# Expert feedforward: router logits written with tokens on partitions, x stationary and the router's columns moving

## The reference, cut to what matters

```python
gate_base = xf @ Wg.T
up_base = xf @ Wu.T
base_out = silu(gate_base) * up_base @ Wd.T
router_logits = xf @ Wr.T                       # (tokens, 8)
probs = softmax(router_logits, axis=-1)
topw, topi = top_k(probs, 2)
...
h = silu(gate_base + g_lora) * (up_base + u_lora)   # for each expert
acc + (h @ Ad_e.T @ Bd_e.T * SCALING) * we[:, None]
```

## Time and profile before

| | |
|---|---|
| time, median of three runs | 2139.03 us (2136.92 to 2142.73) |
| the profiled execution, its own time | 2141.15 us |
| its span, first to last instruction | 2139.4 us |
| mean granted TensorE clock | 0.915 of 2.4 GHz |
| PE busy | 1819.8 us, 85% |
| PEld busy | 1374.9 us, 64% |
| DVE busy | 1452.1 us, 68% |
| ACT busy | 956.3 us, 45% |
| POOL busy | 509.6 us, 24% |

### The profile page before, as it was taken

The page is one execution under the profiler, slowest core; times in us unless marked ns, Lnnn a source line. Parts: engine busy times, 40 slices in busy tenths (PEclk is TensorE's granted clock), DMA queues, the critical chain, the costliest instruction groups (busy, mean ns, idle before and its releaser), DMA issues. The chain is left out here.

```text
span 2139.4 us, 32688 instructions
## 1 busy us (share of the span) xinstructions
PE 1819.8 (85%) x12270; PEld 1374.9 (64%) x12270; DVE 1452.1 (68%) x2729; ACT 956.3 (45%) x1614; POOL 509.6 (24%) x503
## 2 busy tenths in 40 slices
PE   4489999765668999999999985999997799857886
PEld 2256665213448999999999975777875577623443
DVE  8478887694745566566566554566665677648997
ACT  3436666402314444444444432433443211259995
POOL 5233331270010010010000001001100388723422
PEclk9679999656889999999999997999998999978998
DMA  5598894217622122222221214211211311030000
GB/s 157 51 98 96 96 97 45 99 66 230 205 79 57 55 64 69 75 67 63 80 72 56 67 48 162 104 70 40 90 60 54 118 50 50 21 123 6 20 22 34
DMA packets 117568, 166.53 MB, mean 78 GB/s; under 512 B 13536, under 2 KB 67680, under 8 KB 115104
## 3 DMA queue, kind: packets, MB, share of 16 engines
q1 hardware_dynamic: 110756, 151.85, 29.9%
q10 hardware_dynamic: 6656, 12.58, 1.6%
HBM read 117.91 MB, written 21.05 MB: 65 GB/s over the span
## 5 line engine op out<-in xcount | busy, mean ns | idle before, releaser
L1583 ACT ACTIVATE f_gate<-f_gu 128x256 f32<-128x256 f32 x264 | 98.2, 381 | 274.3 <-PE f_gu L1449 187.1
L1711 DVE TENSOR_TENSOR f_hid<-f_gate,f_gu 128x256 f32<-128x256 f32 x264 | 108.2, 420 | 162.6 <-ACT f_gate L1583 159.7
L567 DVE TENSOR_REDUCE a_rowmax<-a_ring 128x2 f32<-128x512 f32 x256 | 164.9, 687 | 51.7 <-PE a_ring L649 49.4
L2525 PE MATMUL e_py<-e_kv,e_toep 128*128 128x320 f32 x640 | 174.5, 436 | 7.5 <-DVE e_kv L2549 7.5
L2525 PEld LDWEIGHTS e_py<-e_kv,e_toep 128*128 128x128 f32 x640 | 122.7, 192 | 59.0 <-issue 9.1
L520 ACT ACTIVATE a_prob<-a_sT 128x1024 f32<-128x1024 f32 x128 | 130.6, 1026 | 48.0 <-PE a_sT L638 48.0
L1462 PE MATMUL f_gu<-f_lowh,f_bg 128*128 128x256 f32 x704 | 141.3, 283 | 5.2 <-POOL f_lowl L1368 4.9
L1449 PE MATMUL f_gu<-f_xhi,f_wg 128*128 128x256 f32 x704 | 130.5, 283 | 0.0
L1449 PE MATMUL f_gu<-f_xhi,f_wu 128*128 128x256 f32 x704 | 129.1, 281 | 0.0
L1716 DVE TENSOR_TENSOR f_hl<-f_hid,f_hh 128x768 fp32r<-128x768 f32 (+2 forms) x90 | 84.5, 939 | 55.9 <-ACT f_hh L1629 54.8
L1462 PEld LDWEIGHTS f_gu<-f_lowh,f_bg 128*128 128x128 f32 x704 | 115.6, 191 | 9.7 <-POOL f_lowl L1368 5.2
(11 more groups left out here) (420 smaller groups left out, 4853.5 us busy)
## 6 DMA issues: line engine op xcount, KB each, us to landing
f_entry<-in_WdT SPq DMA_DIRECT2D x89, 256.0 KB
d_staging<-in_w SPq DMA_DIRECT2D x16, 1024.0 KB, 5.5
a_qs<-a_hi SPq DMA_DIRECT2D x64, 128.0 KB, 7.2
a_ks<-a_hi SPq DMA_DIRECT2D x64, 128.0 KB, 6.2
e_toep<-lags SPq DMA_DIRECT2D x32, 256.0 KB, 3.1
f_entry<-in_Bg SPq DMA_DIRECT2D x89, 64.0 KB
f_entry<-in_Bu SPq DMA_DIRECT2D x89, 64.0 KB
cf<-in_xT SPq DMA_DIRECT2D x4, 1024.0 KB, 7.8
```

The source lines that it names most:

```text
L567: dve.tensor_reduce(rowmax[:, s % 2, :, e * SLOTS + j], ring[n % RING][:, :].rearrange("p (q t) -> p q t", t=T), AX.X, ALU.max, negate=Tru ...
L1583: act.activation(gate[:, i % 2, :], gu[n % 3][:, 0, :], ACT.Silu).then_inc(s_["gate_ready"], 1)
L1711: dve.tensor_tensor(hid[:, j, :], gate[:, i % 2, :], gu[n % 3][:, 1, :], ALU.mult).then_inc(s_["hid_ready"], 1)
L2525: last = pe.matmul(py[n % RING][:, 0:DIAG * BS], toep[:, h % 3, (t - j) * P:(t - j + 1) * P], kv[:, h % 2, :, j, :], start=(j == 0), stop= ...
```

## The change

`logits` now writes the 16 columns with tokens on partitions at once: for each half q of the block and each k, the stationary operand is the 128x128 piece of `raw_x` and the moving one is `wr[:, k, :]` with its 8 columns. `turn_logits`, `fetch_logits`, the tile `f_logitT`, the item "lgT" of the bank's order and the semaphores `lgT_done` and `lgT_ready` go. `logits` stays where it was (s = 3, and ahead of base(0) in the first block); `route_start` stays at s = 5. `grow` waits for `lg_done` where it waited for `lgT_done`.

```diff
-    PREPARE = ("x0", "x1", "lgT", "lg", "z0", "z1", "mk0", "mk1", "low")
+    PREPARE = ("x0", "x1", "lg", "z0", "z1", "mk0", "mk1", "low")
...
                 def logits(b):
-                    claim("lgT", b)
+                    claim("lg", b)
                     pe.wait_ge(s_["raw_ready"], (b + 1) * TB)
-                    for k in range(KT):
-                        last = pe.matmul(misc[0:E_, 0:T], wr[:, k, :], raw_x[:, k, :], start=(k == 0), stop=(k == KT - 1))
-                    last.then_inc(s_["lgT_done"], 1)
-
-                def turn_logits(b):
-                    claim("lg", b)
-                    pe.wait_ge(s_["lgT_ready"], b + 1)
                     for q in range(TB):
-                        last = pe.matmul(misc[:, q * E_:(q + 1) * E_], logitT[:, q * P:(q + 1) * P],
-                                         keep["ident"][0:E_, 0:E_], start=True, stop=True)
+                        for k in range(KT):
+                            last = pe.matmul(misc[:, q * E_:(q + 1) * E_], raw_x[:, k, q * P:(q + 1) * P], wr[:, k, :],
+                                             start=(k == 0), stop=(k == KT - 1))
                     last.then_inc(s_["lg_done"], 1)
...
                 logits(0)
                 base(0)
-                turn_logits(0)
                 base(1)
...
                     if ahead and s == 3:
                         logits(b + 1)
-                    if ahead and s == 4:
-                        turn_logits(b + 1)
...
-                def fetch_logits(b):
-                    act.wait_ge(s_["lgT_done"], b + 1)
-                    act.activation(logitT[:, :], misc[0:E_, 0:T], ACT.Copy).then_inc(s_["lgT_ready"], 1)
-                    act.wait_ge(s_["lgT_ready"], b + 1)
-                    act.sem_inc(s_["misc_read"], 1)
...
                 x_raw(0, 1)
-                fetch_logits(0)
...
-                    if ahead and s == 4:
-                        fetch_logits(b + 1)
...
                 def grow(b):
                     dve.wait_ge(s_["lo_ready"], b + 1)
-                    dve.wait_ge(s_["lgT_done"], b + 1)
+                    dve.wait_ge(s_["lg_done"], b + 1)
```

More of the change, by code:

```diff
@@ L1316, in expert_feedforward @@
         weigh = mk.sb("f_weigh", [P, 2, 2, T])
-        logitT = mk.sb("f_logitT", [E_, T])
         route = mk.sb("f_route", [P, 8, TB * E_])
@@ L1333, in expert_feedforward @@
         raw_low = raw[:, :].rearrange("p (j w t) -> p j w t", j=2, w=2)
-        names = ("rank_made", "x_turned", "raw_ready", "hi_ready", "lo_ready", "misc_read", "lgT_done", "lgT_ready", "lg_done",
+        names = ("rank_made", "x_turned", "raw_ready", "hi_ready", "lo_ready", "misc_read", "lg_done",
                  "lg_ready", "exp_ready", "route_steps", "grown_ready", "masks_turned", "masks_ready", "a_done", "low_ready",
```

## The result

The changed kernel takes 2131.28 us (median of nine runs, 2126.22 to 2133.42), where the kernel before took 2136.92 us over its nine runs (2132.50 to 2142.73); the ratio is 0.9971, with a 95% interval of 0.9958 to 0.9984. Measured again with two other sets of runs it was 0.9958 (0.9943 to 0.9973) and 0.9961 (0.9949 to 0.9973). So 6 to 9 us are gained, 0.29% to 0.42% of the time, where 4.7 us and most likely "within 0.3%" were forecast. The profiled execution took 2133.42 us.

What follows compares the result with a forecast made beforehand. PE was taken to bound the kernel in the later blocks; -4.0 us there and -0.7 in the first block sum to -4.7, from the median of 2139.03 to 2134.4 us, range 2131 to 2140, about 8 in 10.

Steps and rivals of the forecast that it cites:

- PE sets the pace of the seven later blocks: From 655 to 1270 us PE is busy 612.3 of 615 us; what it no longer issues comes off the time.
- `turn_logits` costs 0.62 us: Later blocks: distance from `base` to `down` 0.74 us with it, 0.12 without; removal saves 4.3 us over seven blocks.
- `logits` after: 1.87 us from its first record to `down`, 0.05 more than before: Later blocks: 16 records, 0.11 us apart, take 1.87 us against 1.82; 0.35 us more for seven blocks.
- The first block: -0.7 us: First token block: +0.1 for `logits` at half clock, -0.62 for `turn_logits`, -0.17 for the wait ahead of `turn_masks`.
- the clock rises later: First block: short records don't help raise the clock, base(0) runs slow longer; costs 1.7 us, 2136.0 us; chance 0.22.
- both bounds of the unknown cost: New `logits`, per record: 0.11 us (the loads' pace) or 0.25 us (each waits out the one before); 0.11 taken.
- nothing arriving: The 4.7 us are lost again at a later wait; 2139.0 us; chance 0.10.
- Short records that wait for each other: New `logits`: records adding to the same columns need 0.25 us each; 18 us more, 2152 us; chance 0.05.
- a clock that falls in the later blocks: Short records bring a clock dip of 3.4 us in each of seven blocks; 24 us in all, 2158; chance 0.05.
- moving columns alone: New `logits`: 8 moving columns set the pace, 0.4 us for 1.9; 10 us more than the sum, 2124; chance 0.03.
- A dip less: The shifted start escapes the clock dip from 646 to 656 us; 3.4 us go, 2131 us; chance 0.05.
- The load's time: First block: loads follow the clock, 0.22 us at half, 0.11 at full, against the page's 107 ns whatever the clock.

Runs made afterwards that it cites:

- the short group: Changed kernel with 24 fp32 matmuls (48 records of 8 moving columns, results overwritten) added ahead of the stage's first transpose; one run, 2128.99 us.
- the probe with 8 columns loaded: Changed kernel with two fp32 matmuls added ahead of `down` in four steps, loads 8x128, 128x128, 64x128, 128x8 (this one at s = 0); one run, 2147.75 us.
- padding with zeros: Kernel before, old logits form, router's columns padded from 8 to 128 and logits' rows from 8 to 128; 0.9979 of before.

## Why the prediction came out as it did

- **PE sets the pace of the seven later blocks.** Right. What PE lost in its records came off the steps to 0.02 us, no later wait took it back, and removing ACT's copy and moving nothing else left the other steps alike.
- **`turn_logits` costs 0.62 us.** The step that failed first: the measure ended at the first record of `down`. Its second record was late as well, by 0.11 us, and the cost was 0.73 us, 0.8 us more over seven blocks. The timeline of before had this row.
- **`logits` after: 1.87 us from its first record to `down`, 0.05 more than before.** The mis-sized term, and the larger miss. The pace of 0.11 us a record was right (fourteen distances of 0.11), but the ends of the group were taken from `turn_logits`: the gap of 0.21 us ahead of it, 0.13 between its first two records and 0.18 behind the last. They belong to its load of 8 rows. With full loads these are 0.12, 0.03 and 0.11 us, and the second record of `down` comes 0.02 us sooner, so the group is 0.28 us shorter than in the sum: 0.23 less than before and not 0.05 more. The forecast put the ends down to "the change of kind of matmul". The transposes, which the earlier trace rows show for their pace, already spoke against this reading: another kind too, but with full loads, and the first starts 0.12 us behind the last record of `base` (734.86 - 734.74), without a gap. Seven times 0.28 is 2.0 us.
- **So the later blocks** gave -6.7 us and not -4.0.
- **The first block: -0.7 us.** Not seen. The three parts of the sum did come, at about -1.0 us: `logits` takes 3.41 us up to `base` where it took 3.50 (0.1 less, and not 0.1 more), `turn_logits` went, and the routing chain started early (DVE copied the logits at 627.49, 9.0 us after the first transpose and not 13.0), which brought no more than the short wait ahead of `turn_masks`, as said. But the rival "the clock rises later" came true and took them back: the rise came 12.9 to 14.3 us after the first transpose and not about 10. The block up to the masks came out at +0.7 us, so the late rise cost some 1.7 us, just its price; since that price was borrowed from another dip and halved, so close a hit is luck. Its argument for was right, its argument against (the loads fill the time) is refuted by the short group that ran for 10.4 us at half clock. How much of the +0.7 is left at the stage's end stays open.
- **Sum.** -6.7 us and between 0 and +0.7 make -6.7 to -6.0. The stage took 5.7 to 6.2 us less in the traces, the medians differ by 5.6 us, and by 8 to 9 in the two repetitions, whose intervals reach down to 5.8 us; what the repetitions have beyond 6.7 us was not traced. The forecast of -4.7 and "within 0.3%" erred by two terms of opposite sign, of which the larger one was missing from the list of unknowns: both bounds of the unknown cost lay on the side of dearer records, and none below it on the ends of the group. That 2131.28 us lies just inside the range of 2131 to 2140 is luck: the range was opened for a later rise and for nothing arriving, and no rival had cheaper ends of the group.
- **Short records that wait for each other, a clock that falls in the later blocks, moving columns alone:** none occurred. The pace is 0.11 us, and the clock is 1.00 from 655 to 1270 us. A dip less did not come either: all three traces of the changed kernel have the dip behind the first block, 6.8 us at half clock in two of them, as before, and 3.4 in the third, whose stage was no shorter for it. On moving columns alone, the probe with 8 columns loaded shows that some 0.03 us a record is reached, but only with a narrow load. The Trainium skill's floor of some 25 ns ("TensorE: Matmul & The Clock Gate", section "Back-to-back issue gap") fits that one. The 2126 to 2127 us that the forecast set beside this floor is not worked out there: as an estimate by the floor, 16 records are 0.4 us, the rival's own figure, which gave 2124.
- **The load's time.** The Trainium skill's rule ("TensorE: Matmul & The Clock Gate", section "LDWEIGHTS (loading the stationary operand)") is that the columns of the load count and its rows do not. The probes agree, 0.11 us for 8, 64 and 128 rows alike. Its one formula for either clock does not hold here: the 48 short records took 10.38 us at half clock, 0.21 us each.

## What to carry to other kernels

Cost a small group of matmuls by the distance from the last record ahead of it to the second record behind it, not by its own records: a group whose loads leave rows or columns of the array empty paid some 0.3 us more at its ends here, between full ones (0.29 with 8 or 64 rows, 0.30 for the old `logits` with 8 columns), and padding with zeros took that away. When two forms of a product compete, look which of them fills the loads before counting columns. And where PE starts cold, a stretch of short records can be as long as a streaming one and still leave the clock at 1.2 GHz.

## What the runs showed of the hardware that was not expected

- A matmul with a load of 8 or 64 rows or of 8 columns behind one with a full load starts 0.21 us after it instead of 0.12, and its load starts no sooner; with 8 or 64 rows, the next full matmuls bring the sum to 0.29 us over four records. Among themselves part-filled loads do start early (0.21 us ahead of the matmul in the old `logits`).
- Short records run at the pace of the load's columns: at full clock 0.11 us for 128, about 0.03 for 8.
- 48 records of 8 moving columns, 10.38 us of PE shown as busy without a break, left the clock at 1.2 GHz; as many with 256 columns saw it rise to 2.4 GHz after 5.4 us.
